# Local attention: two operations of the reciprocal root behind each of the first four mask operations, instead of one behind each of eight

## The reference, cut to what matters

```python
def l2norm(t):
    return t / jnp.clip(jnp.linalg.norm(t, axis=-1, keepdims=True), 1e-12)
...
def _layer(x, wqkv, qs, ksc, wo, lg, lb, w1, b1, w2, b2):
    h = shift_token(x)
    q, k, v = jnp.split(h @ wqkv, 3, axis=-1)          # to 8 heads of 64
    q = l2norm(q) * qs
    k = l2norm(k) * ksc
    q, k = rotary_xpos(q, k)
    o = local_attention(q, k, v)      # windows of 128: a query sees its window and the one before
    x = x + o @ wo
    ...                                # the MLP
```

## Time and profile before

| | us |
|---|---|
| median of 3 runs | 2179.41 (2178.56 to 2180.12) |
| the profiled execution, its own time | 2177.43 |
| its span from first to last instruction | 2175.6 |
| PE busy | 1994.9 (92%) |
| DVE busy | 1556.9 (72%) |
| ACT busy | 1090.1 (50%) |
| POOL busy | 414.4 (19%) |

### The profile page before, as it was taken

How to read it: one execution, slowest core, us unless ns; L and a number is a source line. 1 busy time by engine, 2 the same in 40 slices (tenths; PEclk the granted TensorE clock), 3 DMA queues, 4 the chain that set the end, 5 groups by cost and what they waited for, 6 DMA issues and landing times. The chain is left out here.

```text
span 2175.6 us, 43248 instructions
## 1 busy us (share of the span) xinstructions
PE 1994.9 (92%) x13920; PEld 1708.5 (79%) x13920; DVE 1556.9 (72%) x4621; ACT 1090.1 (50%) x2533; POOL 414.4 (19%) x257
## 2 busy tenths in 40 slices
PE   6799999999999967999999969995999999968998
PEld 6678878878878856888888758884888888857887
DVE  5536636645645657999999757775889999957777
ACT  3332222222323226888888734442777777753343
POOL 0100000000000003444444300001444444420010
PEclk9899999999999989999999989998999999988999
DMA  7100000000000020000000010002000000000002
GB/s 257 49 1 1 1 2 1 1 2 1 1 2 1 1 103 2 6 6 5 5 5 5 5 61 11 10 10 64 5 5 5 5 5 6 5 15 15 11 10 82
DMA packets 43266, 42.77 MB, mean 20 GB/s; under 512 B 8514, under 2 KB 37913, under 8 KB 43164
## 3 DMA queue, kind: packets, MB, share of 16 engines
q1 hardware_dynamic: 41030, 36.17, 5.2%
q10 hardware_dynamic: 2134, 5.26, 0.6%
HBM read 33.02 MB, written 8.39 MB: 19 GB/s over the span
## 5 line engine op out<-in xcount | busy, mean ns | idle before, releaser
L887 ACT ACTIVATE l_probs<-l_probs,l_negmax 128x256 f32<-128x256 f32 x512 | 253.1, 496 | 64.9 <-DVE l_negmax L968 64.9
L115 PE MATMUL ps<-local_w_hi,l_xT 128*128 128x512 f32 x384 | 167.1, 435 | 37.1 <-DVE l_xT L961 31.1
L841 POOL TENSOR_TENSOR l_t<-l_t,l_t 128x1024 f32<-128x1024 f32 x64 | 152.9, 2389 | 195.3 <-DVE l_t L1014 195.3
L392 ACT ACTIVATE attn_exp<-ps 128x512 f32<-128x512 f32 x130 | 77.7, 598 | 205.9 <-PE ps L117 205.9
L115 PE MATMUL ps<-attn_w_hi,attn_xT_hi 128*128 128x512 f32 x392 | 168.8, 431 | 12.7 <-issue 10.1
L845 POOL TENSOR_TENSOR l_t<-l_t,l_rnorm 128x1024 f32<-128x1024 f32 x64 | 121.9, 1905 | 307.3 <-DVE l_rnorm L985 307.3
L893 ACT ACTIVATE l_probsT<-ps 128x512 f32<-128x512 f32 x256 | 138.3, 594 | 50.4 <-PE ps L1112 50.4
L116 PE MATMUL ps<-attn_w_lo,attn_xT_hi 128*128 128x512 f32 x392 | 158.5, 404 | 0.0
L117 PE MATMUL ps<-attn_w_hi,attn_xT_lo 128*128 128x512 f32 x392 | 158.1, 403 | 0.0
L117 PE MATMUL ps<-local_w_hi,l_xT 128*128 128x512 f32 x384 | 155.0, 404 | 0.0
L116 PE MATMUL ps<-local_w_lo,l_xT 128*128 128x512 f32 x384 | 154.6, 403 | 0.0
(11 more groups left out here) (212 smaller groups left out, 5859.1 us busy)
## 6 DMA issues: line engine op xcount, KB each, us to landing
tok_x<-x SPq DMA_DIRECT2D x16, 512.0 KB, 4.2
m_shifted<-shifted SPq DMA_DIRECT2D x20, 256.0 KB, 2.8
shifted<-x SPq DMA_DIRECT2D x64, 64.0 KB, 1.5
out<-x SPq DMA_DIRECT2D x8, 512.0 KB, 4.4
ffn_w_raw<-ffn_w SPq DMA_DIRECT2D x6, 640.0 KB
local_w_raw<-ffn_wqkv SPq DMA_DIRECT2D x4, 768.0 KB, 5.3
h<-txt SPq DMA_DIRECT2D x4, 512.0 KB, 4.6
attn_w_raw<-attn_Wq ACTq DMA_DIRECT2D x1, 1024.0 KB, 6.4
```

The source lines that it names most:

```text
L115: nc.tensor.matmul(out, wh, mh, start=start, stop=False, skip_group_check=True)
L392: nc.scalar.activation(ex[:, at % 2], ps[:, at % 2], ACT.Exp).then_inc(s.attn_exp.sem, 1)
L841: nc.gpsimd.tensor_tensor(t1[:], t1[:], t2[:], ALU.add).then_inc(s.summed.sem, 1)
L887: last = nc.scalar.activation(v, v, ACT.Exp, bias=nb[:, h:h + 1], scale=-1.0, accum_out=rsum[:, h:h + 1])
```

## The change

Behind a mask operation DVE now runs up to two operations of the root instead of one, as long as some are left. Operations 3 to 10 thus stand behind mask operations 0 to 3, and nothing stands behind mask operations 4 to 7. The same instructions are issued, with the same waits in front of each; only the order on DVE differs. The streams of the other engines are as before.

```diff
+                k = 3
                 for h in range(LH):
                     if b:
                         if h % 4 == 0:
...
                             nc.vector.memset(idle[:], 0.0)
                         score(n - 1, h, mask)
-                    if a:
-                        chain.wait()
-                        if 3 + h < LAST:
-                            chain.mark(rnorm(3 + h))
-                        else:
-                            rnorm(LAST).then_inc(s.rnorm.sem, 1)
+                    for _ in range(2):
+                        if a and k <= LAST:
+                            chain.wait()
+                            if k < LAST:
+                                chain.mark(rnorm(k))
+                            else:
+                                rnorm(LAST).then_inc(s.rnorm.sem, 1)
+                            k += 1
```

## The result

The changed kernel takes 2204.24 us (median of 4 runs, 2203.32 to 2209.29) against 2179.76 for the one before (2178.56 to 2180.29): 1.0118 times the time, 95% interval 1.0100 to 1.0135, so 24.5 us more. The profiled execution took 2204.13 us, its span is 2202.3 us, 26.7 more than before.

The account below looks back on a forecast made before the run. Loop one, through POOL and PE, was taken to bound the kernel, a second through ACT's squares close behind. Exponentials 0.68 us later cost 29.7 us over 28 pairs, less 2 at layer ends: 2205.1 profiled, 2207 us median; range 2196 to 2215, widened to 2188–2218.

Parts of the forecast that it names:

- Loop one: Scores, masks with the root between them, POOL, PE, scores; PE waits 0.31 us a step for POOL's product L845.
- odd steps: Steps starting with mask_odd, 13.25 us before; forecast 13.64 us, from 12.96 + 0.68.
- The second loop: Masks, exponentials, ACT's copies and squares L907, DVE's rotation L1009, sums, root, masks; slack 0.05 us even, at most 0.29 odd.
- The third pair: Third pair of exponentials on ACT, waiting for masks five and six; to start at 3.55 us of the step instead of 2.87.
- The lower bound: ACT's delay is 0.49 us instead of 0.68 if DVE's boundary waits run beside the root's exposed wait; total 2196 us.
- Even steps: Steps starting with mask_even, 13.25 us before; forecast 13.88 us, from 13.20 + 0.68.
- PE has room for its part: PE needs no more than before and waits a little for ACT and DVE instead of POOL.
- the third: Loop not priced in the forecast: exponentials, L899 and L893 on ACT, L1001 on DVE, PE, scores, masks.
- the ends of the layers: Step behind each layer's last window: POOL released 1.08 us earlier, -2 us in all; first steps left at nothing.
- the one without an exposed wait: Rival: a second root operation on DVE costs only 0.09 us, so no change, 2181 us; chance 0.06.
- the gain by loop one: Rival: PE gets its 0.31 us because L1009 does not move with the exponentials; 2169 us, chance 0.09.
- masks blocked by POOL: Rival: mask operations 5 to 8 must wait for POOL's L845, 120 us more, 2299 us; chance 0.05.

Follow-up runs that it names:

- 1,1,1,1,1,2,1,0: The changed kernel with these numbers of root operations behind masks 1 to 8; 2172.5 us, 0.9967 of the kernel before.
- 2,2,1,1,1,1,0,0: The changed kernel with these numbers of root operations behind masks 1 to 8; 2189.6 us, 1.0037 of the kernel before.
- the held product: The changed kernel with POOL's product L845 made to wait for the sixth mask operation; 2208.0 us, 1.0123 of the kernel before.

## Why the prediction was right

The forecast was 2207 us; measured are 2204.24. Point by point:

- **Loop one bound the kernel, 0.31 us a step to gain.** Shown: the wait is gone with the change, and with the root 0.22 us earlier and the exponentials untouched (1,1,1,1,1,2,1,0) the odd steps fall to 13.00 to 13.03 us.
- **The second loop with 0.05 and at most 0.29 us of slack, held by L907.** That L907 holds it is shown: L1009 names L907 in the changed kernel, and ACT's delay alone reproduces the steps. The 0.05 holds. The "at most 0.29" of the odd step was wrong: DVE is ready for the masks 0.14 us after L961's start, so at 967.02 in the earlier trace rows, and the slack up to 967.39 is 0.37.
- **0.21 us for a dependent root operation, 0.64 a group, 0.35 a bare mask.** All three as measured. From L984 to L985, which waits for it, are 0.21 us, from L985 to the next mask 0.09. The Trainium skill ("VectorE: DVE Perf Modes", section "The DRAIN you can't avoid") says of a chain of eight copies that the semaphore costs nothing extra; for these short operations the rows do not bear that out. The 0.12 us between 0.21 and 0.09 are the price of semaphore and dependence together, as no run has the one without the other.
- **The third pair at 3.55, ACT 0.68 us later.** Measured 3.53 and 0.67 to 0.68. The lower bound, 0.49, had supposed that DVE's waits at the boundary run beside the exposed one; they do not: the step over the boundary is 0.80 us in the changed kernel (960.37 to 961.17) against 0.62 before.
- **Even steps 13.88, odd steps 13.64.** Measured 13.84 to 13.86 and 13.55. The odd one was mis-sized by 0.09: I had the masks start at the end of L961, and they start 0.14 us after its start, 0.08 before its end. This is the same slip as with the 0.29, worth 28 x 0.09 = 2.5 us, and it is the largest error of the steady part. Together 26.1 instead of 29.7 us.
- **PE has room for its part.** Only just: PE's scores come 0.05 to 0.09 us before they would be late. Had the second loop not been there, the third would have taken nearly all of the same time. The text said that PE "waits a little". From start to start, as its 0.31 us of before were counted, it waits 0.69 us for L1001 in the odd step, and in the even one 0.51 for L1001 and 0.31 more ahead of the second transposes of the probabilities: more than twice as long as before, and covered all the same.

The last term, the ends of the layers at -2 us, was wrong in sign. The windows of the first two steps and the last of a layer, summed over both layers, of the kernel before:

```profile
sum 80.40, PE 68.00 PEld 58.17 DVE 54.69 ACT 59.19 POOL 28.46; mean PE 17.00 PEld 14.54 DVE 13.67 ACT 14.80 POOL 7.11
```

The same windows of the changed kernel:

```profile
sum 81.87, PE 69.40 PEld 59.31 DVE 57.22 ACT 59.72 POOL 27.20; mean PE 17.35 PEld 14.83 DVE 14.30 ACT 14.93 POOL 6.80
```

They cost 1.5 us more. The gain that was forecast did come: in the step behind the last window PE's wait for POOL is 2.17 us in layer 0 and 2.13 in layer 1, where it was 3.16. But ACT is late in this step too, and the sum had left that out. PE of the changed kernel, that step of layer 1:

```profile
1948.18 1.06 PE L1152 MATMUL ps<-ident,l_t 128*128 128x128 f32 x8 [2.13 <-POOL l_t L845]
...
1951.03 0.39 PE L115 MATMUL ps<-local_w_hi,l_oT_hi 128*128 128x256 f32 x1 [0.91 <-DVE l_oT_lo L1001]
```

What PE wins at POOL it loses at L1001, and the step takes 13.25 us, 13.16 before. In layer 0 it did gain, 14.80 to 13.73 us, with the granted clock at 0.88 before and after. The two last steps together won 1.0 us instead of 2.

The rest is in the first two steps of each layer, which the prediction had left at nothing. Here are their windows, layer 0 and layer 1, of the kernel before (the number behind POOL's is TensorE's mean granted clock in the window, as a share of full speed):

```profile
835.78:861.56 25.78, 22.53 (x168) 18.82 (x170) 21.53 (x79) 21.06 (x57) 10.88 (x6) 1.00 0.02 4
1519.63:1546.29 26.66, 23.83 (x168) 20.01 (x170) 21.66 (x79) 19.90 (x55) 10.89 (x6) 0.94 0.01 4
```

And of the changed kernel:

```profile
834.92:862.48 27.56, 23.93 (x168) 20.13 (x170) 21.91 (x78) 21.41 (x57) 10.66 (x6) 0.94 0.02 4
1532.63:1559.96 27.33, 23.70 (x168) 20.05 (x170) 21.92 (x79) 20.28 (x55) 10.65 (x6) 0.94 0.01 4
```

At the same granted clock, in layer 1, the change costs 0.67 us. In layer 0 it is 1.78, but there the clock was 1.00 before and 0.94 after. In the kernel before, 1.00 in one layer and 0.94 in the other go with 25.78 and 26.66 us, so about 0.9 of the 1.5 us may be the clock that one profile happened to catch; that the change itself lowers it is not excluded. In the same way the last step of a layer takes 12.94 and 14.33 us in the two layers of one and the same kernel (2,2,1,1,1,1,0,0), at a granted clock of 1.00 and 0.88. A term of 2 us can't be read from one trace there.

The errors of the steady part (-3.6) and of the ends (+3.5) cancel, so that the sum for the profiled execution, +27.7 us, lies 1.0 from the measured +26.7: that is luck. The other 1.9 us of the distance come from the median, which I had put 2.0 us above the profiled execution and which lies 0.1 above it. The mechanism was right, and the distance of 3 us flatters the sum. Of the rivals, the one without an exposed wait falls by the 0.21 us, the gain by loop one by the kernel with ACT made later, and masks blocked by POOL by the held product and by their length: 0.42 us beside L845 as without it.

## What to carry to other kernels

Where an engine works between two producers of another engine's work, count what each group of its instructions delivers against what the consumer takes: here 0.86 us a pair against ACT's 0.99 left 0.13 us of slack a pair, and one exposed wait of 0.21 spends more than that. A chain of small dependent operations belongs one by one between independent ones; to end it earlier, double it up where the consumer is behind, not where it is waiting. And when a wait on the critical path is taken away, look for every loop that closes through the moved work: here three lay within 0.4 us of each other, so that removing 1.1 us from one could give at most 0.3, and pushing 0.7 into the others took 0.5.

## What was not expected of the hardware

POOL's spread of the reciprocals L833 and DVE's L1001 change lengths with their order. In the odd step of the changed kernel, L992 and L1001 from the timeline of DVE:

```profile
963.16 0.88 DVE L992 TENSOR_SCALAR l_mask_even<-l_mask_prev,l_negs 128x128 f32<-128x128 f32 x1
...
964.62 1.55 DVE L1001 TENSOR_TENSOR l_oT_lo<-l_oT,l_oT_hi 128x512 fp32r<-128x512 f32 x1 [0.18 <-ACT l_oT_hi L899]
```

Beside them POOL, in the timeline of the same kernel:

```profile
963.10 0.85 POOL L855 TENSOR_TENSOR ffn_w_lo<-ffn_w_raw,ffn_w_hi  x1
964.58 1.04 POOL L833 TENSOR_TENSOR l_spread<-l_rowinv,l_one 128x512 f32<-128x512 f32 x1 [0.63 <-DVE l_rowinv L997]
```

L992 took 1.61 us in the kernel before and ended with POOL's L845; now it takes 0.88 and ends at 964.04, with L855 (963.95). L1001 took 0.95 us before, when it started 0.37 us ahead of L833 (960.30 and 960.67), and L833 took 1.48. Now L833 starts 0.04 us ahead, takes 1.04, and L1001 takes 1.55 and ends 0.55 after it. This reads as if the one that starts first keeps the other out for as long as it runs; no run here measured it by itself. In the kernel with ACT made later, where L833 is nearly over when L1001 starts (they share 0.10 us), L1001 takes 0.69 us. What L992 wins and L1001 loses is covered in the odd step by ACT, as L1009 starts 0.29 us after the end of L907 (965.97) as in every step of the loop; the cover is thin, as L1001 ends only 0.09 us ahead of L1009's start. PE's wait for L1001 is where it nearly shows.
